# Half of phase 1 woven into the gate scan and the first mixer group of a fused mLSTM-mixer and MoE kernel

## The chip, the cores and the metric

The kernel runs on one core of a Trainium2 chip. The metric is the time of one execution on the device in microseconds. Five instruction queues run side by side and meet only at semaphores: TensorE (PE), VectorE (DVE), ScalarE (ACT), GpSimd (POOL) and the queue that issues the transfers (SP). Each queue executes its instructions in the order in which they were written.

## What is computed

A block of two layers on x of 8 sequences x 1024 tokens x 128 channels, in float32. The first is an mLSTM mixer:

```python
x_mlstm, z = jnp.split(x @ W_up, 2, axis=-1)
x_act = swish(conv4(x_mlstm) + conv_b)               # causal, 4 taps, per channel
q, k, v = headwise(x_act, Wq), headwise(x_act, Wk), headwise(x_mlstm, Wv)
ig, fg = [q, k, v] @ W_ig + b_ig, [q, k, v] @ W_fg + b_fg
lfc = cumsum(log_sigmoid(fg))                        # over the tokens
logD = where(mask, lfc_i - lfc_j + ig_j, -inf);  mD = max(logD, axis=-1)
C = (q @ k.T) * DH ** -0.5 * exp(logD - mD)
h = C / (max(abs(C.sum(-1)), exp(-mD)) + 1e-6) @ v   # 4 heads of 64
h_state = (norm(h) * norm_w + skip * x_act) * swish(z)
x = layernorm(x + h_state @ W_down)
```

The second is an FFN with 16 experts of width 64, of which the 4 best by a sigmoid gate are weighed per token, and a shared expert of width 128: `x = layernorm(x + shared + routed)`.

## The kernel before

The 8192 tokens are cut into 16 groups of G = 512, two to a sequence ("batch" b, "half" f). Four stages follow one another.

**Phase 1** (`phase1`, one function per queue) goes through the 8 batches, 16 halves. SP loads a half of x (`x_in`, L382). PE transposes it into bank 0 (`phase1_xt`, L1190). ACT copies that into `x_hi` and `x_t` (L638, L639), and DVE takes `x_lo = x_t - x_hi` (`x_low`, L815). PE multiplies by W_up in three products each for four blocks of columns (`phase1_up`, L1200 to L1204) into banks 1 to 4. ACT copies the first two into `xm` (L650) and puts the second two through Silu (L673, the gate z). DVE runs the four taps of the convolution on `xm` in pairs of instructions (L835 the first, L838 the others), ACT puts the result through Silu (`phase1_xact`, L628), PE adds the products for the gates into bank 5 (`gate_rows_of`, L1164), and SP stores `xact` (1 MB) and `x_t` to scratch in HBM (L374, L386). On the PE, ACT and DVE queues neighbouring halves overlap: `x_low` of the next half is between the taps of this one.

**The gate scan** runs once over all 8 batches together, on 128 rows (4 chunks x 8 batches x 4 heads). ACT and DVE turn bank 5 into log gates and running sums and maxima (L773 to L778, L852 to L869), PE and DVE carry these from chunk to chunk (L1439 to L1449, L876 to L889), PE spreads the maxima and inter-chunk weights of group 0 over the partitions (L1453, L1462), and three sets of rows go back into token order (`back`, L1434, L902, L904). For the later groups, maxima, weights and decays go through HBM: SP stores them (`store_rows`, L426) and loads them group by group (`load_max`, L404, 1 MB, `load_inter`, L408).

**The groups** (`groups`, L319): `mix(0, None)`, a loop with `mix(g, g - 1)` for g from 1 to 14, `mix(15, 14)`, and `ffn(15)`. `mix(g, f)` carries the mixer of group g beside the FFN of group f. Group 0 has no FFN beside it. In a mixer group POOL makes the arguments of the decay matrices (`args`, L538, L548) and scaled queries (`weigh_queries`, `qs`, L558), ACT exponentiates the former (`decays`, L707), and PE and DVE go through four chunks in a chain: scores times decays on DVE (`weigh_scores`, L934, "C"), keys times weights (`weigh_keys`, L940, "K"), the products of the chunk on PE (`chunk`, L1313 to L1320), the state on DVE (`update_state`, L951, "S"), and POOL's next `kept` (L567). Then come the head scale ("R", L959 to L971, and L580 and L583 on POOL), the head transposes (`head_transposes`, L1329, "H"), the gating by z on DVE (`gate_heads`, L979, L983), the down projection (`down`, L1339, "D"), the sum y (L1008), its statistics and the normalised Y (L1002). `mix_front(g + 1)` prepares keys, values and first scores of the next group. The FFN of a group goes through `ffn_slot(f, j)` for ten slots j; the tables `PE_SLOT` and `DVE_SLOT` (L1483 to L1486) say after which slot each mixer step is issued. The routing takes part of the first slots.

At the first FFN product (L1366) of group 0, PE has `ffn_head`, `key_tokens` and `ffn_logits` of `mix(1, 0)` behind it.

Of the kernel before, what the change touches and what calls it, by code (L numbers as in the profile page):

```python
# [31 lines left out]
F32R = mybir.dt.float32r  # L32
BF16 = mybir.dt.bfloat16
ALU = mybir.AluOpType
# [3 lines left out]
P = 128  # L38
# [5 lines left out]
def mixer_moe_block(nc, x, W_up, conv_w, conv_b, Wq, Wk, Wv, W_ig, b_ig, W_fg, b_fg, norm_w, skip,  # L44
# [18 lines left out]
    QD = Wq.shape[1]  # L63
    assert E == P and INNER == 2 * P and DH == 64 and NH == 4 and HX == 64 and HALVES == 2
# [9 lines left out]
    with ExitStack() as ctx:  # L74
# [81 lines left out]

        p1 = ExitStack()
# [21 lines left out]
        min_f = sb1("min_f", [P, HALVES, P])  # L179
        pre_i = sb1("pre_i", [P, HALVES, P])  # L180
        abs_f = sb1("abs_f", [P, HALVES, P])
        exp_f = sb1("exp_f", [P, HALVES, P])
        log_f = sb1("log_f", [P, HALVES, P])
        p1.close()


        lfc = sb("lfc", [P, HALVES, P])
        rows_a = sb("rows_a", [P, HALVES, P])
        own_max = sb("own_max", [P, HALVES, P])
        run_max = sb("run_max", [P, HALVES, P])  # L190
        ends = sb("ends", [P, 2, HALVES])
        end_rows = sb("end_rows", [R, NC, 2, HALVES])
        carry_rows = sb("carry_rows", [R, CS + 1])
        carry = sb("carry", [P, HALVES])
        neg_end = sb("neg_end", [P, HALVES])
        rows_w = sb("rows_w", [P, HALVES, P])
        rows_floor = sb("rows_floor", [P, HALVES, P])
        rows_inter = sb("rows_inter", [P, HALVES, P])
        rows_decay = sb("rows_decay", [R, CS])
        end_max = sb("end_max", [R, CS])  # L200

# [21 lines left out]
        rows_stored = sem("rows_stored")  # L223
        decay_in = sem("decay_in")
# [3 lines left out]
        x_res = sb("x_res", [P, NC, E])  # L228
        u_sb = sb("u_sb", [P, NC, NH, DV])
        sq = sb("sq", [P, 2, NH, DH])  # L230
        ssq = sb("ssq", [P, NC, NH])
        nrm = sb("nrm", [P, NC, NH])
        nrm1 = sb("nrm1", [P, NC, NH])
        nrm2 = sb("nrm2", [P, NC, NH])
        var_h = sb("var_h", [P, NC, NH])
        r_h = sb("r_h", [P, NC, NH])
        half = sb("half", [P, NC * NH])
        hn = sb("hn", [P, NC, INNER])
        mixed = sb("mixed", [P, NP, G])
        y1 = sb("y1", [P, NC, E])  # L240
        st1 = sb("st1", [P, NC, 6])
        mv1 = sb("mv1", [P, NC, 2])
        ve1 = sb("ve1", [P, NC])
        rs1 = sb("rs1", [P, NC])
        Y = sb("Y", [P, NC, E])
        yT = sb("yT", [P, G])
        yT_hi = sb("yT_hi", [P, G], F32R)
        yT_lo = sb("yT_lo", [P, G], F32R)
        ge = sb("ge", [P, NC, NX])
        ge1 = sb("ge1", [P, NC, NX])  # L250
        gext = sb("gext", [P, NC, NX + TOPK])
        top = sb("top", [P, NC, 8])
        rest = sb("rest", [P, NC, NX + TOPK])
        chosen = sb("chosen", [P, NC, NX])
        csum = sb("csum", [P, NC])
        crec = sb("crec", [P, NC])
        comb = sb("comb", [P, NC, NX])
        comb2 = sb("comb2", [P, NC, 2 * NX], F32R)
        combT = sb("combT", [P, G], F32R)
        s_in = sb("s_in", [P, 2, G])  # L260
        h1 = sb("h1", [P, 2, G])
        h2 = sb("h2", [P, 2, G])
        z2 = sb("z2", [P, NC, E])
        st2 = sb("st2", [P, NC, 6])
        mv2 = sb("mv2", [P, NC, 2])
        ve2 = sb("ve2", [P, NC])
        rs2 = sb("rs2", [P, NC])
        out_sb = sb("out_sb", [P, NC, E])
# [50 lines left out]
        def groups(eng, mix, ffn):  # L319
# [6 lines left out]
            ffn(NG - 1)  # L326

# [13 lines left out]
        def _(sp):  # L341
# [53 lines left out]
            with sp.Fori(FFN_DMAS // HALVES, B - 1) as b:  # L395
                phase1(b)
            phase1(B - 1)
            store_xact(B - 1, 1)

            sp.wait_ge(xt_stored[0], 16 * B)  # L400
            sp.dma_start(xT2[:], xt_d[0]).then_inc(xT_in, 16)
# [13 lines left out]
            sp.wait_ge(xact_stored[0], 16 * B)  # L415
            load_xa(0)
# [6 lines left out]
            def store_rows(dram, rows, s, f):  # L423
                by_chunk = dram.rearrange("(b f) h (k t) -> f k b h t", f=HALVES, k=NC)
                for k in range(NC):
                    sp.dma_start(by_chunk[f, k], rows[k * R:(k + 1) * R, f]).then_inc(s, 16)  # L426

            load_z(0)
            sp.wait_ge(act_scan, SCAN_DECAY_EXP)
            sp.dma_start(decay_d.rearrange("h b c -> b h c"), rows_decay[:]).then_inc(rows_stored, 16)  # L430
            sp.wait_ge(rows_stored, 16)
            for par in range(2):
                for p in range(NP):
                    sp.dma_start(decay[par * DH:(par + 1) * DH, p, :],
                                 decay_d[2 * p + par].rearrange("b c -> (b c)").partition_broadcast(DH)
                                 ).then_inc(decay_in, 16)
# [1091 lines left out]
```

## Time and profile before

| | |
|---|---|
| median of 3 runs | 862.72 us (862.7 to 867.3) |
| profiled execution | 864.57 us, span from first to last instruction 862.8 us |
| mean granted TensorE clock | 0.963 of full speed |
| busy: PE, DVE, ACT, POOL | 787.7, 644.4, 363.7, 371.7 us |
| HBM read, written | 55.24 MB, 25.43 MB |

The page of the profile gives, for the span, each engine's busy time, 40 slices with the granted clock, and groups of instructions. A group of the loop (for instance from one set of transposes L1348 at 219.87 us to the next at 263.68) takes 42 to 44 us. Matmuls overlap and each is drawn with its full duration, so a PE that is drawn busy isn't at its peak; the distance between starts says what one costs in a stream.

### The profile page before, as it was taken

Reading aid. Unit: us, or ns where it says so; the run is one execution under the profiler, and the core shown is the slowest. Engines: PE = TensorE matmul, PEld = TensorE weight load, DVE = VectorE, ACT = ScalarE, POOL = GpSimd, SP = SyncE. Lnnn points to the kernel's source line nnn. Section 1 sums busy time; section 2 is a strip of 40 time slices with the busy share of each in tenths; the row PEclk is TensorE's granted clock in tenths of the full one; section 3 lists DMA queues with packets and bytes.
Section 4 is the critical chain, followed back from the end, with each engine's and each line's share of the span. In section 5 each row is a group of like instructions: output and inputs, shape, how many; then the busy total and the mean of one; then the engine's idle time right before and its main releaser. Section 6 shows DMA issues by size and latency. Waiting matters only on the chain.

```text
span 862.8 us, 17647 instructions
## 1 busy us (share of the span) xinstructions
PE 787.7 (91%) x5783; PEld 666.1 (77%) x5783; DVE 644.4 (75%) x1711; ACT 363.7 (42%) x621; POOL 371.7 (43%) x370
## 2 busy tenths in 40 slices
PE   6888968689999999999999999999999999999976
PEld 5656656578888888888888798888898888888855
DVE  5799953377778777777777877777878777778754
ACT  4757833143434343434343434343434343434131
POOL 5050008553455455454545544545455454543200
PEclk8999977599999999999999999999999999999979
DMA  4887744030404040404040405040404040400000
GB/s 121 237 259 262 288 177 127 30 123 25 135 24 134 24 134 24 134 24 134 24 132 26 134 24 132 26 133 25 134 24 134 24 134 24 134 24 25 1 13 13
DMA packets 53104, 81.01 MB, mean 94 GB/s; under 512 B 10176, under 2 KB 36952, under 8 KB 49112
## 3 DMA queue, kind: packets, MB, share of 16 engines
q1 hardware_dynamic: 53080, 80.68, 30.4%
q8 instruction: 16, 0.26, 0.1%
q14 instruction: 8, 0.07, 0.0%
HBM read 55.24 MB, written 25.43 MB: 93 GB/s over the span
## 4 chain that ended last, share of the span: by engine, by line
PE 45%; DVE 19%; issue 15%; DMA 9%; POOL 6%; ACT 2%; SPq 2%; POOLq 1%; DVEq 1%; ACTq 0%
PE bank L1395 11%; DMA max_b<-max_scratch 8%; PE bank L1366 5%; PE bank L1370 5%; PE bank L1367 5%; DVE acc L838 5%; PE bank L1339 3%; DVE st L990 3%; PE bank L1315 3%; PE bank L1385 3%; PE bank L1313 2%; PE bank L1320 2%; DVE Y L1002 2%; POOL D L548 2%; POOL D L538 2%
## 5 line engine op out<-in xcount | busy, mean ns | idle before, releaser
L754 ACT ACTIVATE s_in<-bank 128x512 f32<-128x512 f32 x144 | 86.1, 598 | 175.9 <-PE bank L1370 174.8
L1395 PEld LDWEIGHTS bank<-ewout,h 128*128 128x128 f32 x1024 | 132.8, 191 | 8.5
L1366 PE MATMUL bank<-yT_hi,in_hi 128*128 128x512 f32 x288 | 128.0, 444 | 8.3 <-DVE h L1097 8.3
L1395 PE MATMUL bank<-ewout,h 128*128 128x128 f32 x1024 | 134.9, 275 | 0.0
L1097 DVE TENSOR_TENSOR h<-s_in,bank 128x512 f32<-128x512 f32 x144 | 98.2, 682 | 49.0 <-PE bank L1370 42.2
L552 POOL TENSOR_TENSOR rs<-ve,half 128x4 f32<-128x4 f32 x32 | 32.6, 1019 | 206.6 <-DVE ve L998 206.6
L1370 PE MATMUL bank<-yT_lo,in_hi 128*128 128x512 f32 x288 | 114.3, 397 | 0.0
L1367 PE MATMUL bank<-yT_hi,in_lo 128*128 128x512 f32 x288 | 113.9, 395 | 0.0
L538 POOL TENSOR_TENSOR D<-a_tok,max_b 128x512 f32<-128x512 f32 x64 | 65.4, 1043 | 110.7 <-DVE max_b L910 67.8
L1101 DVE TENSOR_TENSOR h<-h,bank 128x512 f32<-128x512 f32 x128 | 87.2, 681 | 14.4 <-PE bank L1385 14.4
L951 DVE TENSOR_TENSOR state<-kept,bank 64x130 f32<-64x130 f32 x128 | 36.6, 286 | 59.1 <-PE bank L1320 29.6
L619 ACT ACTIVATE u_sb<-bank 128x260 f32<-128x260 f32 x64 | 24.8, 388 | 131.1 <-PE bank L1315 131.1
L567 POOL TENSOR_TENSOR kept<-state,decay 128x260 f32<-128x260 f32 x64 | 39.7, 620 | 89.0 <-DVE state L951 88.8
L1315 PE MATMUL bank<-vals,C 128*128 128x65 f32 x512 | 73.9, 269 | 0.0
L1366 PEld LDWEIGHTS bank<-yT_hi,in_hi 128*128 128x128 f32 x288 | 55.1, 191 | 20.9 <-DVE h L1097 15.2
L1315 PEld LDWEIGHTS bank<-vals,C 128*128 128x128 f32 x512 | 70.5, 199 | 0.0
L580 POOL TENSOR_TENSOR r_h<-var_h,half 128x8 f32<-128x8 f32 x32 | 52.9, 1653 | 40.2 <-DVE var_h L971 39.1
L838 DVE SCALAR_TENSOR_TENSOR acc<-xm,vecs,acc 128x512 f32<-128x512 f32 x96 | 68.2, 780 | 0.0
L1370 PEld LDWEIGHTS bank<-yT_lo,in_hi 128*128 128x128 f32 x288 | 54.6, 190 | 12.9
L1313 PE MATMUL bank<-state,qs 128*128 128x130 f32 x256 | 56.6, 304 | 7.5 <-issue 5.2
L1367 PEld LDWEIGHTS bank<-yT_hi,in_lo 128*128 128x128 f32 x288 | 55.4, 192 | 5.3
L1313 PEld LDWEIGHTS bank<-state,qs 128*128 128x128 f32 x256 | 41.2, 197 | 16.5 <-issue 15.3
(193 smaller groups left out, 1623.6 us busy)
## 6 DMA issues: line engine op xcount, KB each, us to landing
xact_scratch<-xact SPq DMA_DIRECT2D x16, 1024.0 KB, 4.8
max_b<-max_scratch SPq DMA_DIRECT2D x15, 1024.0 KB, 7.8
xa<-xact_scratch SPq DMA_DIRECT2D x16, 512.0 KB, 6.2
silu_z<-xact_scratch SPq DMA_DIRECT2D x16, 512.0 KB, 3.8
inter_w<-inter_scratch SPq DMA_DIRECT2D x30, 256.0 KB, 7.1
x_in<-in_L_attn_x_dram SPq DMA_DIRECT2D x16, 256.0 KB, 4.8
xt_scratch<-x_t SPq DMA_DIRECT2D x16, 256.0 KB, 4.9
xT<-xt_scratch SPq DMA_DIRECT2D x16, 256.0 KB, 8.2
```

The lines of the kernel that those rows point to most:

```text
L538: pool.tensor_tensor(D[:, kp, par], a_g.rearrange("p k (s two) -> p two k s", two=2)[:, par, 2 * kp:2 * kp + 2] .unsqueeze(3).to_broadcast ...
L580: pool.tensor_tensor(r_h[:, c].rearrange("p k h -> p (k h)"), var_h[:, c].rearrange("p k h -> p (k h)"), half[:, 0:2 * NH], ALU.pow).then_ ...
L754: act.activation(s_in[:, j % 2], bank[4][:], ACT.Silu).then_inc(silu_done, 1)
L838: i = dve.scalar_tensor_tensor(a, src, vecs[:, p, t:t + 1], a, ALU.mult, ALU.add)
L1097: dve.tensor_tensor(dst[:, j % 2], s_in[:, j % 2], bank[5][:], ALU.mult).then_inc(h1_done, 1)
L1101: dve.tensor_tensor(h2[:, (j - 1) % 2], h1[:, (j - 1) % 2], bank[6][:], ALU.mult).then_inc(h2_done, 1)
L1313: pe.matmul(o, qs[:, p, c], state[:, p], start=True, stop=False, skip_group_check=True)
L1315: i = pe.matmul(o[:, par * DV:(par + 1) * DV], C[:, par, kk, p], vals[:, k, 2 * p + par], start=False, stop=True, skip_group_check=True)
L1366: pe.matmul(o, in_hi[:, m, j], yT_hi[:], start=True, stop=False)
L1367: pe.matmul(o, in_lo[:, m, j], yT_hi[:], start=False, stop=False)
L1370: pe.matmul(o, in_hi[:, m, j], yT_lo[:], start=False, stop=True).then_inc(done, 1)
L1395: i = pe.matmul(bank[7][:, k * P:(k + 1) * P], h2[:, j % 2, k * P:(k + 1) * P], w, start=(j == k == 0), stop=(j == NJ), skip_group_check=True)
```

## The change

Phase 1 as it was now runs over the first EARLY = 4 batches only. The other eight halves are "late halves" h = 0 to 7. Their instructions are written by hand into the queues of the scan and of `mix(0)`:

- DVE: a late half is five steps (tap 0, `x_low` of the next half, taps 1 to 3), 40 in all. `late(n)` issues the next n: 3 ahead of the scan, 1, 4, 2, 1 and 3 between its parts, then 1 ahead of the first keys, 14 ahead of the steps of `mix(0)` by `LATE_STEPS`, 5 ahead of the head gating, 6 ahead of y.
- PE: `late_first(h)` (transposes of half h + 1 into bank 7, first two products of half h), `late_second(h)` (the other two) and `late_gates(h)`. All four products of a half use the two banks 4 and 6 in turn.
- ACT: `late_xm`, `late_xt`, `late_xact` and `late_z`.
- SP: `late(h)`: load of a half of x, stores of `x_t` and `xact`, between the transfers of `mix(0)`.

The scan runs twice, first over batches 0 to 3, of which groups 0 to 7 are made; the second pass (s = 1) is spread out: the gate rows after y of group 0, chunk scans in slot 3 of group 1, ends in slot 5, carry in slots 6 and 7, the exponentials at the end of group 1, and the rows back in slot 5 of group 2, with the stores by SP there. Groups 0, 1 and 2 are written out ahead of the loop, which goes from 3 to 14. Banks of the scan's small results move. Tiles that live beyond phase 1 no longer share memory with it; this changes no instruction.

The core of the diff (the functions of the scan are cut out of the old text and get a parameter s; those lines are left out):

```diff
+    EARLY = B // 2
+    LATE = HALVES * (B - EARLY)
...
-            mix(0, None)
-            with eng.Fori(1, NG - 1) as g:
+            for g in range(SCAN_GROUPS):
+                mix(g, g - 1 if g else None)
+            ready()
+            with eng.Fori(SCAN_GROUPS, NG - 1) as g:
                 mix(g, g - 1)
...
+        # SP
+            late(0, False)
+            sp.wait_ge(xt_stored[0], 16 * EARLY)
+            sp.dma_start(xT2[:], xt_d[0]).then_inc(xT_in, 16)
+            sp.wait_ge(xact_stored[0], 16 * EARLY)
             load_xa(0)
             load_z(0)
+            sp.dma_start(x_res[:], x_g[0]).then_inc(x_res_in, 16)
+            store_xact(EARLY - 1, 1)
+            late(1, False)
+            store_decay(0)
+            store_maxima(0, 1)
+            late_xact(1)
+            load_decay(0)
+            late(2)
+            store_maxima(0, 0)
...
+                    elif isinstance(g, int) and g == 2:
+                        store_decay(1)
+                        store_maxima(1, 0)
+                        store_maxima(1, 1)
+                        load_decay(1)
...
+        # ACT
+            late_xm(0)
+            late_xt(0)
+            late_z(0)
+            late_xact(0)
             act.preload_act_table_set("natural_log_exp_and_others")
+            scan_gates(0)
+            late_xm(1)
+            scan_ends(0)
+            late_xt(1)
+            scan_rows(0)
             act.wait_ge(max_mm, 1)
             for h in (2, 3):
                 copy(max_b[:, h], bank[(1, 2, 3, 0)[h]][:]).then_inc(max_in, 4)
+            late_z(1)
             act.wait_ge(inter_mm, 1)
+            copy(inter_w[:, 0], bank[3][:]).then_inc(inter_in, 16)
+            late_xact(1)
+            late_xm(2)
             mix_front(0)
             decays(0)
+            late_xt(2)
+            late_xact(2)
+            late_z(2)
...
+            def late_steps(k):      # k == NC: after the loop over the slots
+                if k == 0:
+                    late_xm(3)
+                elif k == 1:
+                    late_xt(3); late_xact(3); late_z(3)
+                elif k == 2:
+                    late_xm(4); late_xt(4); late_xact(4); late_z(4)
+                elif k == 3:
+                    late_xm(5)
+                else:
+                    late_xt(5); late_xact(5); late_z(5)
+                    late_xm(6); late_xt(6); late_xact(6); late_z(6)
+                    late_xm(7); late_xact(7); late_z(7); late_xact(8)
+                    scan_gates(1)
...
+        # DVE
+            late(3)
+            scan_gates(0)
+            scan_chunks(0)
+            late(1)
+            scan_carry(0)
+            scan_maxima(0)
+            back(0, 0)
+            late(4)
             dve.wait_ge(max_mm, 1)
             for h in (0, 1):
                 dve.tensor_copy(max_b[:, h], bank[(1, 2, 3, 0)[h]][:]).then_inc(max_in, 4)
+            late(2)
+            back(0, 1)
+            back(0, 2)
+            late(1)
             dve.wait_ge(inter_mm, 1)
+            dve.tensor_copy(inter_w[:, 1], bank[0][:]).then_inc(inter_in, 16)
+            late(3)
...
+        # PE
+            late_first(0)
+            phase1_gates_x(EARLY - 1, 1)
+            phase1_gates(EARLY - 1, 0)
+            late_second(0)
+            phase1_gates(EARLY - 1, 1)
+            late_first(1)
...
+            scan_ends(0)
+            back(0, 0)
+            late_gates(1)
+            scan_carry(0)
...
             i.then_inc(max_mm, 1)
+            late_second(1)
+            back(0, 1)
+            back(0, 2)
...
             i.then_inc(inter_mm, 1)
+            late_first(2)
             mix_keys(0)
             mix_values(0)
+            late_gates(2)
+            late_second(2)
...
+            def late_steps(what, arg):
+                if (what, arg) == ("C", 0):
+                    late_gates(3); late_second(3)
+                elif (what, arg) == ("C", 1):
+                    late_first(4)
+                elif (what, arg) == ("K", 1):
+                    late_gates(4); late_second(4)
+                elif (what, arg) == ("C", 2):
+                    late_first(5)
+                elif (what, arg) == ("C", 3):
+                    late_gates(5); late_second(5); late_first(6)
+                elif what == "H":
+                    late_gates(6); late_second(6)
+                elif (what, arg) == ("D", 1):
+                    late_first(7); late_gates(7); late_second(7)
...
+LATE_UP = (4, 6)
+LATE_STEPS = {("S", 0): 3, ("S", 1): 2, ("C", 1): 2, ("K", 1): 2, ("S", 2): 1, ("S", 3): 4, ("H", None): 5}
+SCAN_GROUPS = 3
+SCAN_CHUNKS_SLOT, SCAN_ENDS_SLOT, SCAN_CARRY_SLOT, SCAN_MAX_SLOT, SCAN_BACK_SLOT = 3, 5, 6, 7, 5
```

In the excerpt several calls are put on one line, some waits are left out, and the lines "# SP" and the like name the queue. On PE, `late_first(3)` is ahead of the first chunk of `mix(0)`, behind `key_tokens`. `late_up` waits for a bank to be free, `late_xt(h)` is the copy of the transposes of half h + 1, and `late_xact(h)` is the Silu after the taps of half h - 1.

## Rows read from the trace of the kernel before

**Rows 1.** Busy time by stage: window, length, engines (instructions), granted clock, DMA.

```profile
70.00:114.00 44.00, 40.11 (x529) 28.33 (x527) 44.00 (x73) 32.63 (x64) 0.00 (x0) 0.98 0.77 275
114.00:179.00 65.00, 45.66 (x303) 38.70 (x304) 26.82 (x76) 20.13 (x39) 32.09 (x34) 0.68 0.38 121
179.00:222.00 43.00, 41.39 (x289) 35.75 (x290) 32.69 (x93) 17.93 (x29) 21.68 (x21) 1.00 0.10 29
```

**Rows 2.** Chain of waits, whole span (start, length, what): two batches of phase 1.

```profile
87.28 0.92 DVE acc L835 x2
88.79 2.74 DVE acc L838 x5
98.26 0.92 DVE acc L835 x2
```

**Rows 3.** Timeline of PE (start, duration): one half of phase 1.

```profile
88.48 0.66 PE L1190 MATMUL bank<-ident,x_in 128*128 128x128 f32 x4
88.89 0.48 PE L1200 MATMUL bank<-x_hi,up_hi 128*128 128x512 f32 x1
...
90.45 0.64 PE L1164 MATMUL bank<-x_t,g_pad 128*32 128x128 f32 x16
91.02 0.50 PE L1200 MATMUL bank<-x_hi,up_hi 128*128 128x512 f32 x1
...
92.62 1.08 PE L1164 MATMUL bank<-xact,g_pad 128*32 128x128 f32 x32
```

**Rows 4.** Timeline of ACT, the scan.

```profile
114.82 1.28 ACT L768 ACT_TABLE_LOAD   x1
...
128.06 1.09 ACT L619 ACTIVATE max_b<-bank 128x512 f32<-128x512 f32 x2 [5.08 <-PE bank L1453]
```

**Rows 5.** Chain of waits from 100 to 180 us.

```profile
113.60 1.21 ACT xact L628 x2
...
121.77 0.49 DVE run_max L888 x2
...
122.30 5.67 PE bank L1453 x32
...
138.91 0.46 PE bank L1313 x2
...
158.53 0.29 DVE state L951
```

**Rows 6.** Timeline of PE: the first FFN product of group 0.

```profile
178.85 0.47 PE L1366 MATMUL bank<-yT_hi,in_hi 128*128 128x512 f32 x1
```

**Rows 7.** Windows of 2 us, PE: busy time, then the granted clock.

```profile
116.00:118.00 2.00, 0.00 (x0) 0.50 1.14 352
126.00:128.00 2.00, 2.00 (x19) 0.96 0.11 26
140.00:142.00 2.00, 1.87 (x9) 0.50 0.95 244
```

**Rows 8.** Timeline of POOL: arguments and queries of group 0.

```profile
129.51 2.04 POOL L538 TENSOR_TENSOR D<-a_tok,max_b 128x512 f32<-128x512 f32 x2 [67.77 <-DVE max_b L910]
...
132.71 2.38 POOL L558 TENSOR_TENSOR qs<-xa,inter_w 128x1024 f32<-128x1024 f32 x1
```

**Rows 9.** Timeline of DVE: scan, copies of max_b, sum y of group 0.

```profile
117.64 0.74 DVE L859 TENSOR_TENSOR_SCAN lfc<-min_f,log_f 128x128 f32<-128x128 f32 x2
...
128.07 1.29 DVE L910 COPY max_b<-bank 128x512 f32<-128x512 f32 x2 [4.89 <-PE bank L1453]
...
170.89 0.69 DVE L1008 TENSOR_TENSOR y<-bank,x_res 128x512 f32<-128x512 f32 x1 [3.75 <-PE bank L1339]
```

**Rows 10.** Timeline of DVE in phase 1 while POOL works.

```profile
55.82 3.11 DVE L815 TENSOR_TENSOR x_lo<-x_t,x_hi 128x512 fp32r<-128x512 f32 x1
58.86 6.45 DVE L838 SCALAR_TENSOR_TENSOR acc<-xm,vecs,acc 128x512 f32<-128x512 f32 x6
```

**Rows 11.** Timeline of POOL in the same stretch.

```profile
55.59 5.85 POOL L525 TENSOR_TENSOR in_lo<-in_w,in_hi 128x1152 fp32r<-128x1152 f32 x2
```

More of the change, by code:

```diff
@@ L437, in _ @@
[L437 to L448 removed]
+                    r = k * R + part * n
@@ L452, in mix @@
             def mix(g, f):
+                first = isinstance(g, int) and g == 0
+                if isinstance(g, int) and g == 1:
+                    for i in range(HALVES):
+                        sp.wait_ge(xt_stored[i], 16 * B)
+                        sp.wait_ge(xact_stored[i], 16 * B)
                 sp.wait_ge(arg_sub, nth(g, 4, 3))
@@ L466, in mix @@
                     load_z(g + 1)
+                    if first:
+                        late(7)
                 if f is not None:
@@ L783, in _ @@
-            act.wait_ge(dve_scan, SCAN_MAX)
-            for f in range(HALVES):
-                act.activation(rows_inter[:, f], run_max[:, f], ACT.Exp, scale=-1.0, bias=carry[:, f:f + 1]
-                               ).then_inc(act_scan, 1)
+            scan_gates(0)
[3 more added lines that the diff above has]
+            scan_rows(0)
             act.wait_ge(max_mm, 1)
@@ new lines, in phase1, with late @@
+                    tap(b, f, 0)
+                    if f == 0:
+                        x_low(b, 1)
+                    else:
+                        x_low(b + 1, 0)
+                    for t in range(1, TAPS):
+                        tap(b, f, t)
+            late_done = [0]
+            def late(n):
+                for _ in range(n):
+                    h, step = divmod(late_done[0], TAPS + 1)
+                    late_done[0] += 1
+                    b, f = late_half(h)
+                    if step == 1:
+                        if h < LATE - 1:
+                            x_low(*late_half(h + 1))
+                    else:
+                        tap(b, f, step - (step > 1))
@@ L903, in back @@
+            def back(s, n):
+                dve.wait_ge(back_mm, 2 * BACK if s else n + 1)
+                d = (a_tok, w_tok, floor_tok)[n][:].rearrange("p b f k h -> p f k b h")
+                rows = back_bank(s, n)[:, 0:CS * R].rearrange("p (f k b h) -> p f k b h", f=HALVES, k=NC, b=B)
+                for f in range(HALVES):
+                    if n == 2:
+                        j = dve.tensor_scalar(d[:, f, :, batches(s)], rows[:, f, :, batches(s)], EPS_MIX, None, ALU.add)
                     else:
-                        j = dve.tensor_copy(d[:, f], s[:, f])
+                        j = dve.tensor_copy(d[:, f, :, batches(s)], rows[:, f, :, batches(s)])
@@ L1018, in mix_front, with scan_steps @@
                 weigh_scores(g, 0)
+            def scan_steps(g, j):
+                if g == 1 and j == SCAN_CHUNKS_SLOT:
+                    scan_chunks(1)
+                elif g == 1 and j == SCAN_CARRY_SLOT:
+                    scan_carry(1)
+                elif g == 1 and j == SCAN_MAX_SLOT:
+                    scan_maxima(1)
+                elif g == 2 and j == SCAN_BACK_SLOT:
+                    for n in range(BACK):
+                        back(1, n)
             def mix(g, f):
+                first = isinstance(g, int) and g == 0
+                if first:
+                    late(1)
                 weigh_keys(g, 0)
@@ L1033, in mix @@
                                 if arg is not None else gate_heads(g)
+                if first:
+                    late(6)
                 mixer_out(g)
+                if first:
+                    assert late_done[0] == LATE * (TAPS + 1)
+                    scan_gates(1)
                 if f is not None:
@@ L1211, in phase1 @@
                         phase1_xt(b, 1)
-                    elif not first and not last:
+                    elif not first:
                         phase1_xt(b + 1, 0)
@@ L1413, in mix @@
                 key_tokens(g, 0)
+                if first:
+                    late_first(3)
                 if f is not None:
@@ L1497 @@
 SCAN_INTER = 7
+ACT_SCAN = 10
 BACK = 3
```

617 lines of the change are left out of this document (385 added, 232 removed).

## The prediction

> **What bounds the kernel now.** I read the stage windows first, then the chain of waits from the last batch of phase 1 to the first FFN matmul, then the timelines of single engines there. The kernel has three regimes [rows 1]. From 70 to 114 us, the last four batches of phase 1, DVE is busy for 44.00 of 44 us: the convolution taps set the pace, one batch of two halves per 10.98 us, 5.49 us a half, its taps following one another at 0.55 us (five in 2.74) [rows 2]. From 114 to 179 us (the gate scan and mixer group 0, with no FFN beside it) no engine is full: DVE 26.82 of 65 us, PE 45.66, and much of that at the low clock. From 179 us the groups are full of PE work (41.39 of 43 us). So 38 us of DVE idleness stand beside 44 us of DVE work that group 0 does not need. The change tries to pour the second into the first.
>
> **What is removed.** Eight halves of phase 1 leave the stretch in which they are alone: 8 x 5.49 = 43.9 us [rows 2]. The last half of a batch now has an x_low in it, 0.6 us, which the last of all has not, so the taps of the fourth batch end 43.3 us before those of the eighth do, at 70.3 instead of 113.6 [rows 5]. I call this moment T in both kernels.
>
> **What a late half costs on each engine.** PE [rows 3]: transposes 0.41, first two up products 1.56, gate rows from x 0.57, second pair 1.6, gate rows from xact 1.08 us: 5.2 us at 2.4 GHz, 42 us for eight. DVE: 0.92 for the first tap pair, 0.6 for x_low (from 88.20 to 88.79), 3 x 1.1 for the rest: 4.8 [rows 2]. ACT: four pairs like the 1.09 us of the max_b pair [rows 4], 4.4 us. DMA: the same transfers over a longer time. The sums of the stage are then 26.8 + 8 x 4.8 = 65 us on DVE, and on PE 42 plus between half and all of its present 45.66 (much of that is at 1.2 GHz), 65 to 88, say 75, against the present 43.3 + 65.3 = 108.6 us from T to the first FFN matmul. The sums alone allow a gain near 33 us. But each half goes PE, ACT, DVE, ACT, PE; four in-order queues carry it in a written order, now in the same two product banks (4 and 6) for all four products of a half; and each link can hold back the mixer instruction behind it. So I walk the queues, with T = 0. The times after are mine, from these durations; those before are read from [rows 5, 6, 9], less 113.6.
>
> - *To run_max.* Before 8.2. After: ACT has the second pair of half 0 ahead of the last xact, so the scan begins 1.6 us later; DVE does a pair of taps in the scan's gap. 10.6: +2.4.
> - *To max_b copied.* Before 15.8. The 32 broadcasts take 5.67 us because they start at 1.2 GHz (granted 0.50 at 116, full by 126 [rows 7]) after PE stood idle between two gate groups. After, late products fill that hole and I take 3.7 us; DVE's four queued steps delay its copies by 1 us. 16.6: -1.6 for the stage.
> - *To the first chunk, C0.* Before 25.3. After, POOL's first two arguments end at 19.9. Its qs waits for DVE's copy of inter_w, which stands behind the first tap of half 2, which waits for ACT's xm, which waits for PE (up products behind the inter broadcasts): 23.0. qs (2.4 us) and the other arguments (3.2, as from 129.51 to 132.71) [rows 8] end at 28.6, their exponentials at 29.3, and only then does ACT come to late_xt(2). DVE's late(3) stands ahead of mix_front(0) and needs exactly that x_t for x_low: DVE is idle for 7 us, to 30.4. Then x_low, two tap pairs, vals and the C pair: 35.1. PE meanwhile waits 5 us, falls to 1.2 GHz as it does now after idling, and does key_tokens, late_first(3) and C0 at that rate. C0 at 39: +12.9 for the stage. This is where most of the overlap is lost.
> - *C0 to the last state.* Before 19.9 (25.3 to 45.2). After, each later chunk has one or two up-product blocks before it (1.6 us of PE each), and S, C and K on DVE have 14 steps of about 1 us among them, of which two x_low wait until ACT has evacuated u. I get 29.4 (39 to 68.4): +9.5.
> - *Last state to y.* Before 12.1; after, the last taps of half 5 and four steps of half 6 stand ahead of the head gating, and the rest of half 6 and half 7 ahead of y, the last half waiting for its up products behind D: 20.0 (y at 88.4): +7.9.
> - *y to the first FFN matmul.* Before 8.0. After, scan_gates(1) stands between y and Y on DVE and waits for ACT's last xact, the gate rows and an activation table load (1.28 us [rows 4]); decays(1) and the evacuations of keyT come after it on ACT. 11.5 (to 99.9): +3.5.
>
> Sum: 2.4 - 1.6 + 12.9 + 9.5 + 7.9 + 3.5 = 34.6 us back of 43.3, net -8.7.
>
> **The second scan.** Its DVE part, without the gate rows counted above, is about 6 us: from 117.64 [rows 9] to the end of run_max at 122.26 [rows 5] are 4.6 us with 0.9 of waiting, and the floor and three back copies come on top. Its 14 transposes and small matmuls add 1.5 us of PE to groups that have PE busy for 41.39 of 43 us. Slot 3 of a group has no DVE room, the others some. Between 0 (all hidden) and 7.5 (all shown, DVE and PE) I take the middle, 4. SP's 21 extra issues in group 2 stand behind load_inter and ahead of load_xa, which is needed only at the group's end: 0. Peeling two iterations: 0, between -1 and +1, for I find no pause at the loop's edge to take away.
>
> **A cost between engines.** At 55.8 us one x_low took 3.11 us and at 58.9 six taps 6.45, while POOL ran its two in_lo subtractions, 5.85 us [rows 10, 11]; alone they take 0.6 and 3.3 [rows 2]. So 5.6 us were lost to 5.85 of POOL: POOL instructions with SBUF inputs hold up DVE ones with two SBUF inputs. The rest of phase 1 ran with POOL idle; now the taps meet 32 us of POOL work [rows 1]. If a third of it meets taps, DVE loses 10 us, some of it in waits that exist anyway. Not in the walk: between 0 and 10, I take 1, because the longest POOL runs (the arguments and qs of group 0) fall mostly in DVE's 7 us wait. The Trainium skill (SBUF — State Buffer, Who interferes with whom) says that the shared ports are held for a whole instruction and the loser blocks fully; the trace's 3.11 us agrees. By that rule, applied to all 32 us, the sum would end near the time before; this is rival C.
>
> Total: -8.7 + 4 + 1 = -3.7 us. The profiled execution took 864.6 us (span 862.8); less 3.7 is 860.9, and as the median of the runs is 1.9 us lower, 859.0 as a median. I say **859**.
>
> **Rivals.**
> A. *The overlap works.* The wait of DVE for late_xt(2) is short and the steps between S, C and K fall into DVE's idle time. For it: DVE has 38 us idle there, and the PE clock may stay up. Against it: the order of the queues above. With half the gap between the walk's 34.6 us given back and the sums' 10 us (a stage of 75), 22 come back: 864.6 - 43.3 + 22 + 5 gives 848, **846** as a median.
> B. *Slower: the low clock.* PE stays at 1.2 GHz from C0 to the end of D, as it does now from 140 on although it is busy most of the time [rows 7]. Then five late halves of 5.2 us of PE work cost 10.4 each: +26, of which the walk's idle PE time hides about 8: 861 + 18 = 879, **877**. It decides once PE is low for more than some 15 of those 50 us.
> C. *The gain goes to the shared port.* 10 us instead of 1: 870, **868**, within 1%.
>
> **Numbers.** Forecast 0.40, A 0.33, B 0.12, C 0.12, something else 0.03. A measurement of this kernel tells a change of about 1% (8.6 us) from none. Faster by over 1% (below 854.1): A and a tenth of the forecast's case: 0.37. Slower (above 871.4): B, the rest and a fifth of C: 0.17. Within: 0.46. The range leaves out the better part of A and most of B: 843 to 871; the forecast's own is 851 to 867.
>
> **What would show it.** T at 70 us; run_max 10 us and C0 39 us after it; a DVE wait of some 7 us on ACT's x_t before vals of group 0; a PE clock of 0.5 around C0; y 88 us and the first FFN matmul 99 us after T; groups 1 and 2 together 4 to 5 us longer than two others; taps of 1 to 3 us beside POOL instructions. C0 before 32 us is A; a granted clock of 0.5 for most of C0 to D is B. The prediction is wrong if one of these moves by over 8 us, or if an SP wait (the xact stores stand ahead of store_maxima and load_xa) delays a load that I count as early.

## The result and the profile after

| | before | after |
|---|---|---|
| median of 4 runs each, side by side | 864.51 us | 886.92 us |
| profiled execution, span | 862.8 us | 886.0 us |
| mean granted TensorE clock | 0.963 | 0.966 |
| busy: PE, DVE, ACT, POOL | 787.7, 644.4, 363.7, 371.7 us | 790.5, 659.4, 355.0, 375.4 us |

The changed kernel is slower: ratio 1.0226, interval 1.0176 to 1.0275. The forecast of 859 and its range to 871 missed it, on the side of rivals B and C, but for neither's reason alone. The kernel before took between 864.5 and 871.6 us as a median beside the different runs below, and the changed kernel was timed only here; so an experiment is compared with the changed kernel by the stage times of the profiles, and its ratio stands for itself.

Busy time by stage of the changed kernel (columns as in [rows 1]):

```profile
70.00:114.00 44.00, 33.52 (x323) 26.38 (x321) 30.96 (x64) 27.81 (x52) 13.23 (x14) 0.88 0.47 160
114.00:149.00 35.00, 25.77 (x274) 21.10 (x272) 25.04 (x45) 16.17 (x32) 15.05 (x14) 0.95 0.67 205
149.00:174.00 25.00, 15.36 (x186) 12.56 (x186) 15.21 (x26) 6.99 (x14) 5.56 (x3) 0.80 0.33 125
174.00:190.00 16.00, 9.74 (x78) 7.56 (x79) 8.04 (x22) 10.99 (x19) 3.15 (x3) 0.89 0.55 199
```

No engine is full in any of the four stretches; DVE (the third pair, after PE and PEld) was busy for 44.00 of 44 us in phase 1 before. The work was moved into DVE's idle time, and a new idle time grew around it. The prediction's T, 113.6 in the kernel before, is 3.53 us after the start of the last six taps (110.07), when the first Silu behind them can start. The last six early taps start at 68.03 in the changed kernel, so T is 71.6 there. From these the stages compare as follows, each as its growth over before:

| stage | forecast | measured | ends after at |
|---|---|---|---|
| T to run_max | +2.4 | +4.0 | 83.73 (start) |
| to max_b copied | -1.6 | +0.3 | 91.67 |
| to C0 | +12.9 | +12.4 | 113.57 |
| to the last state | +9.5 | +15.0 | 148.45 |
| to y | +7.9 | +13.6 | 174.11 |
| to the first FFN product | +3.5 | +7.5 | 189.54 |
| sum | +34.6 | +52.7 | |

52.7 us came back for 42.0 removed (the sums are of unrounded times), where 34.6 of 43.3 were forecast. From one set of transposes of Y to the next, group 1 took 48.42 us (43.28 before) and group 2 44.99 (43.81): the second scan shows 6.3 us, where 4 was taken. Groups 3 to 15 took 43.49 on average against 42.99, 6.5 us in all; of those e1 and e7 below tell. Sums: 52.7 - 42.0 + 6.3 + 6.5, and 0.3 at the tail, is 23.8; the spans differ by 23.2, the rest is that the first line ends at the FFN product and the others start at the transposes.

**Where the forecast was right.** Ahead of C0 DVE, ACT and PE wait for one another as walked. DVE and ACT, then PE:

```profile
105.68 0.87 DVE L974 TENSOR_TENSOR x_lo<-x_t,x_hi 128x512 fp32r<-128x512 f32 x1 [7.36 <-ACT x_t L687]
```
```profile
105.66 1.28 ACT L696 ACT_TABLE_LOAD   x1
```
```profile
109.95 1.09 PE L1555 MATMUL bank<-ident,keyT 128*128 128x128 f32 x4 [5.23 <-DVE vals L1123]
```

DVE stands 7.36 us (7 forecast) on the x_t that ACT makes only after the exponentials of D, and PE waits 5.23 us behind it (5 forecast). One term on the way there was wrong: the late products did not keep the clock up for the 32 broadcasts of the maxima. PE waits 2.05 us ahead of the scan's transposes at 81.41, the granted clock is 0.50 from 84 to 88 us, and the broadcasts take 6.01 us, where 3.7 were taken and 5.67 measured before.

**What the walk had not seen.** Four things, in order of time.

First, SP. The chain of waits of the changed kernel from 108 to 124 us:

```profile
108.58 0.69 SPq L452
...
113.28 0.62 SPq L452
113.94 1.75 DMA inter_scratch<-rows_inter
115.84 0.34 SPq L433
116.22 7.78 DMA x_in<-in_L_attn_x_dram
124.04 0.66 PE bank L1412 x4
```
```profile
124.04 0.66 PE L1412 MATMUL bank<-ident,x_in 128*128 128x128 f32 x4 [2.07 <-DMA x_in<-in_L_attn_x_dram]
```

The load of x for late half 5 is issued at 116.22. It stood behind the store of an xact that waited for ACT (108.13), eight stores of the scan's rows (0.6 to 0.7 us each), the wait that they have landed, and the load of max_b; it then took 7.78 us beside the 1 MB of max_b. PE waited 2.07 us for it here; e5 to e7 show a wait of over 7 us once the links ahead of it are shorter. The walk gave SP no stage of its own: it listed a delayed load under what would make it wrong, and the sum has no term for it.

Second, DVE beside POOL. DVE, then POOL:

```profile
131.49 4.68 DVE L989 SCALAR_TENSOR_TENSOR acc<-xm,vecs,acc 128x512 f32<-128x512 f32 x4
136.09 0.68 DVE L1138 TENSOR_TENSOR keys<-bank,w_tok 128x512 f32<-128x512 f32 x1
```
```profile
131.06 2.49 POOL L606 TENSOR_TENSOR D<-a_tok,max_b 128x512 f32<-128x512 f32 x2 [3.79 <-DVE C L1132]
133.51 2.12 POOL L616 TENSOR_SCALAR_AFFINE_SELECT D<-D 128x512 f32<-128x512 f32 x2
```

Four taps take 4.68 us where four take 2.73 when POOL is idle (at 145.10), the keys stand behind them, and PE waits 3.58 us for the keys at 136.83. All taps of L989 together are busy for 75.3 us against 68.2 before.

Third, the head part. PE, DVE, ACT:

```profile
153.38 1.97 PE L1593 MATMUL bank<-ident,hn 128*128 128x128 f32 x8 [5.62 <-POOL hn L651]
155.28 1.08 PE L1386 MATMUL bank<-x_t,g_pad 128*32 128x128 f32 x16
...
164.01 3.62 PE L1603 MATMUL bank<-w_down,mixed 128*128 128x128 f32 x16 [4.76 <-DVE mixed L1181]
```
```profile
157.88 0.69 DVE L974 TENSOR_TENSOR x_lo<-x_t,x_hi 128x512 fp32r<-128x512 f32 x1 [5.71 <-ACT x_t L687]
```
```profile
156.76 0.60 ACT L687 ACTIVATE x_hi<-bank 128x512 fp32r<-128x512 f32 x1 [8.37 <-PE bank L1386]
```

ACT may overwrite x_t only after PE has read it for the gate rows of half 5 (L1386 at 155.28). Those products are queued behind the head transposes, which wait for POOL's hn. So hn holds x_lo of the next half, which holds taps, which hold `mixed`, which holds D. PE falls to the low clock in its two idle stretches (granted 0.80 in this stage). D takes 3.62 us, much as in the kernel before, where it ran at the low clock too:

```profile
167.29 3.56 PE L1339 MATMUL bank<-w_down,mixed 128*128 128x128 f32 x16 [2.14 <-DVE mixed L983]
```

Fourth, table loads, and keyT behind them. ACT, then PE and DVE:

```profile
176.61 1.28 ACT L906 ACT_TABLE_LOAD   x1
178.34 1.28 ACT L908 ACT_TABLE_LOAD   x1
180.07 1.28 ACT L775 ACT_TABLE_LOAD   x1
```
```profile
184.66 2.08 PE L1546 MATMUL bank<-xa,keyT 64*128 64x128 f32 x16 [5.03 <-ACT keyT L687]
```
```profile
186.81 1.29 DVE L1132 TENSOR_TENSOR C<-bank,D 128x512 f32<-128x512 f32 x2 [6.45 <-PE bank L1546]
```

One load of 1.28 us was in the walk; there are three. The first scan's code asks for a table with both functions ahead of the scan, the second pass doesn't, so Exp, Ln and the exponentials of D each bring their own.

And in group 1, where the second scan's carry is. DVE, POOL, PE:

```profile
216.50 2.44 DVE L1060 TENSOR_TENSOR_SCAN carry_rows<-end_rows,carry_rows 32x4 f32<-32x4 f32 x2
```
```profile
216.33 2.34 POOL L626 TENSOR_TENSOR qs<-xa,inter_w 128x1024 f32<-128x1024 f32 x1
```
```profile
218.99 0.24 PE L1748 MATMUL bank<-carry_rows,ident 32*32 32x2 f32 x8 [1.47 <-DVE carry_rows L1060]
223.74 0.50 PE L1630 MATMUL bank<-yT_hi,in_hi 128*128 128x512 f32 x1 [1.79 <-DVE run_max L1077]
```

Two scans of 32x4 elements took 2.44 us in place of 0.46 (the first pass, at 82.59), as long as POOL's qs ran, and PE waited twice.

### The profile page after: what moved, and what is told of

It reads as the page before. It is cut to its first block, busy times and chain, and to the rows that moved or that the text cites. A ratio compares the mean times of both kernels' runs of the same rounds, so it can differ in the third digit from the quotient of the medians.

```text
span 886.0 us, 17398 instructions
## 1 busy us (share of the span) xinstructions
PE 790.5 (89%) x5805; PEld 668.1 (75%) x5805; DVE 659.4 (74%) x1735; ACT 355.0 (40%) x623; POOL 375.4 (42%) x370
## 4 chain that ended last, share of the span: by engine, by line
PE 43%; DVE 17%; DMA 13%; issue 12%; POOL 6%; ACT 4%; SPq 4%; POOLq 1%; DVEq 0%; ACTq 0%
DMA max_b<-max_scratch 11%; PE bank L1659 10%; PE bank L1630 5%; PE bank L1634 5%; PE bank L1631 4%; PE bank L1603 3%; DVE st L1188 3%; PE bank L1649 3%; DVE acc L989 2%; POOL D L616 2%; POOL D L606 2%; PE bank L1593 2%; DMA x_in<-in_L_attn_x_dram 2%; DVE Y L1200 2%; PE bank L1577 2%
## 5 line engine op out<-in xcount | busy, mean ns | idle before, releaser
L1630 PE MATMUL bank<-yT_hi,in_hi 128*128 128x512 f32 x288 | 128.2, 445 | 12.9 <-DVE h L1319 11.1
L989 DVE SCALAR_TENSOR_TENSOR acc<-xm,vecs,acc 128x512 f32<-128x512 f32 x96 | 75.3, 844 | 0.0
L1577 PE MATMUL bank<-vals,C 128*128 128x65 f32 x512 | 71.2, 262 | 0.0
L1577 PEld LDWEIGHTS bank<-vals,C 128*128 128x128 f32 x512 | 67.3, 191 | 0.0
L1575 PE MATMUL bank<-state,qs 128*128 128x130 f32 x256 | 54.8, 296 | 9.0 <-issue 8.0
```

Of the source, the lines that this page charges most:

```text
L989: i = dve.scalar_tensor_tensor(a, src, vecs[:, p, t:t + 1], a, ALU.mult, ALU.add)
L1575: pe.matmul(o, qs[:, p, c], state[:, p], start=True, stop=False, skip_group_check=True)
L1577: i = pe.matmul(o[:, par * DV:(par + 1) * DV], C[:, par, kk, p], vals[:, k, 2 * p + par], start=False, stop=True, skip_group_check=True)
L1630: pe.matmul(o, in_hi[:, m, j], yT_hi[:], start=True, stop=False)
```

## The experiments

The start of `min_f` (78.27 after, 116.73 before) marks a run's own start-up, which differs by some us between executions. "Stage" below is the time from it to the transposes of Y of group 0: 59.9 before, 108.4 after.

**e1: the written-out groups alone.** Kernel before, groups 0 to 2 written out ahead of the loop.

```diff
-            mix(0, None)
-            with eng.Fori(1, NG - 1) as g:
+            for g in range(3):
+                mix(g, g - 1 if g else None)
+            with eng.Fori(3, NG - 1) as g:
```

> The kernel before with groups 0 to 2 written out ahead of its loop, nothing else changed. The changed kernel's groups 3 to 15 take 6.5 us more in all than those of before, 0.5 each. If writing out groups (longer code, other loop bounds) does that, this kernel is 5 to 8 us slower than before. If it is the landing of the max_b load (8.1 us median in the changed kernel, 7.8 before), which varies from execution to execution, this kernel is within 2 us of before.

Ratio 0.9965 (0.9919 to 1.0011). Groups 3 to 15 take 43.34 us on average in its profile, again above the 42.99 of before, with a time that isn't longer. In e11 and e12, whose groups are those of the kernel before, they take 43.34 and 43.55. So the 6.5 us of the loop groups are mostly the scatter of one execution, not the new shape of the program. In e1 a group's period (42.0 to 44.5 us) goes with how long POOL waits for max_b: 44.5 where it waits 4.97 us, 42.0 where it waits 0.61.

**e2: no second scan in groups 1 and 2.** The changed kernel without chunk scans, carry, maxima, exponentials and rows back of pass 1; the gate rows stay. The tokens of batches 4 to 7 get rows of batches 0 to 3.

```diff
-                if g == 1 and j == SCAN_CHUNKS_SLOT:
-                    scan_chunks(1)
...
-                elif g == 2 and j == SCAN_BACK_SLOT:
-                    for n in range(BACK):
-                        back(1, n)
```

> The changed kernel without the second scan pass in groups 1 and 2 (chunk scans, ends, carry, maxima, rows back, their exponentials); its gate rows at the end of group 0 stay. Tokens of batches 4 to 7 get the rows of batches 0 to 3, so part of the computation is left out. Groups 1 and 2 take 6.3 us more than before in the changed kernel. If that is the second pass, this one is 5 to 7 us faster than the changed kernel and group 2 is back at 43 to 44 us; if it is the low clock and the late start of group 1 after the stage, it gains under 3 us and group 1 stays above 46 us.

Ratio 1.0129 (1.0051 to 1.0207). Transposes of Y at 186.65 as with the scan; group 1 43.50 us, group 2 43.91. The second scan costs 4.9 and 1.1, 6.0 us, as the first of the two expectations has it; most of the loss lies ahead of it.

**e3: gate rows of half 5 ahead of the head transposes.**

```diff
                     late_first(6)
+                    phase1_gates_x(*late_half(5))
                 elif what == "H":
-                    late_gates(6)
+                    phase1_gates(*late_half(4))
```

> The changed kernel, but PE adds the gate rows from x_t of half 5 ahead of the head transposes of group 0 and not behind them. In the trace ACT waits 8.4 us for these (they free x_t), DVE then 5.7 us for ACT's x_t, and the head gating of group 0 stands behind that. Theory 'order of the queues': 4 to 6 us faster. Rival 'amount of work' (ports, PE clock and the sum of work set the length, so a wait that is taken away comes back elsewhere): under 1.5 us.

Ratio 1.0078 (1.0035 to 1.0121), stage 103.8: 4.6 us less. x_lo of half 6 now runs at 151.60 with no wait, y at 169.12 in place of 174.11. The third link is shown. Not all of it is kept: the four taps behind this x_lo now run beside POOL's hn and qs and take 5.62 us for 2.73, and group 1 takes 50.18 us for 48.42.

**e4: one table load for the second pass.**

```diff
             def scan_gates(s):
+                if s:
+                    act.preload_act_table_set("natural_log_exp_and_others")
```

> The changed kernel with one table load ahead of the gate rows of the second pass, with Exp and Ln in one table. In the trace ACT does three loads of 1.28 us there (before exp_f, before log_f, before D) and PE waits 5.0 us for keyT behind them. Theory 'order of the queues': the three become one, which hides in ACT's wait for the gate rows: 3 to 4 us faster. Rival 'amount of work': under 1.5 us, since Y of group 0 or the low clock takes over.

Ratio 1.0109 (1.0071 to 1.0148), stage 103.1: 5.3 us less. ACT:

```profile
175.62 1.28 ACT L901 ACT_TABLE_LOAD   x1
176.92 0.47 ACT L905 ACTIVATE abs_f<-bank,b_f 128x256 f32<-128x256 f32 x1
177.43 0.42 ACT L908 ACTIVATE exp_f<-abs_f 128x256 f32<-128x256 f32 x1
```

The one load that is left stands where ACT waits for the last gate rows anyway, so three loads, 3.84 us, leave the path. PE shows most of the rest:

```profile
181.48 1.16 PE L1548 MATMUL bank<-xa,keyT 64*128 64x128 f32 x16 [1.09 <-ACT keyT L687]
```

It waits 1.09 us for keyT in place of 5.03, keeps the full clock, and the 16 products take 1.16 us in place of 2.08. The Trainium skill (ScalarE: Activation LUTs, What ACT_TABLE_LOAD costs) gives a load 1.28 us, as here, plus about 1.4 us of draining; in the changed kernel the exponential ends at 178.32 and the next load starts at 178.34, so no such drain shows.

**e5: DVE's wait ahead of C0 taken away.** `mix_front(0)` and the first keys go ahead of four late steps, and `late_first(3)` behind C0.

```diff
-            late(3)
...
-                if first:
-                    late(1)
                 weigh_keys(g, 0)
+                if first:
+                    late(4)
```

> The changed kernel with the tap steps taken from ahead of vals, C and keys of group 0: mix_front(0) and weigh_keys(0) go first on DVE, late_first(3) behind C0 on PE, late_xm(3) behind the first u on ACT, and the steps ahead of S0 later (none, 3, 2, 2, 3, 4, 5). In the changed kernel DVE waits 7.4 us for ACT's x_t there and C0 starts 41.6 us after the last early tap. Theory 'order of the queues': C0 at 35 us and the kernel 4 to 7 us faster than the changed one (ratio to before near 1.015). Rival 'amount of work': C0 is early but the tap steps, now packed into the chunks, take it back; y stays where it is and the kernel gains under 1.5 us.

Ratio 1.0179 (1.0123 to 1.0235), stage 107.1: 1.3 us less, the size of the rival. The wait of 7.36 us is gone (DVE waits 2.29 for vals) and C comes at 103.27 instead of 109.73, yet the end of the stage hardly moves: PE now waits 7.7 us for x of half 5, 2.07 in the changed kernel. The 7 us that the walk named as "where most of the overlap is lost" are not to be had by themselves, since the same load is late behind them. What they are worth once it comes early no run tells, for e9 has both.

**e6: the three together,** with the chunk scans in slot 4 in place of 3.

> The changed kernel with the gate rows of half 5 first, one table load, the front of group 0 first, and the chunk scans of the second pass in slot 4 (not 3) of group 1. The single steps took 5.0 and 4.1 us off the stage before group 1. Theory 'order': they add up to 12 to 16 us, so the kernel is 3 to 8 us slower than before. Rival: they overlap and give 8 us at most.

Ratio 1.0044 (1.0015 to 1.0073), stage 96.6: 11.8 us less (4.6, 5.3 and 1.3 alone add to 11.2), so the three add up. Group 1 is no better (49.96). The largest waits left, PE and DVE:

```profile
121.61 1.12 PE L1414 MATMUL bank<-ident,x_in 128*128 128x128 f32 x4 [7.90 <-DMA x_in<-in_L_attn_x_dram]
```
```profile
126.21 1.29 DVE L1134 TENSOR_TENSOR C<-bank,D 128x512 f32<-128x512 f32 x2 [9.11 <-issue]
```

**e7 and e8: max_b loaded half a group earlier,** in e6 and in the kernel before. In both, SP loads max_b of group g + 2 as soon as the last arguments of g + 1 are made:

```diff
                     load_xa(g + 1)
+                    if not (isinstance(g, int) and g == NG - 2):
+                        sp.wait_ge(arg_sub, nth(g, 4, 7))
+                        load_max(g + 2)
```

> The four orders and, besides, SP issues load_max(g + 2) in group g as soon as POOL has read max_b, and not behind the output store and x_res of the next group. Groups take 42.1 us where the load lands in time and 43 to 45 where POOL waits for it. If that wait sets the difference, all groups come to 42.1 to 42.4 us and the kernel is 12 to 16 us faster than with the four orders alone; if it is absorbed, under 3 us.

> The kernel before with the early load_max alone (and groups 14 and 15 written out). Its groups take 43.1 us in the mean and 42.1 where the load lands within 7.8 us. Theory 'the load sets the excess': 12 to 14 us faster than before, groups at 42.1 to 42.3. If another wait takes over, under 4 us.

e7: ratio 1.0016 (0.9986 to 1.0046), median 868.45 beside e6's 871.94; every period from group 3 to 14 is 43.0, and POOL no longer waits for the DMA there. e8: ratio 0.9946 (0.9912 to 0.9980), some 4.7 us, periods of groups 2 to 14 from 43.0 to 43.1, where 42.1 was expected. That the landing makes the scatter is shown; neither expected gain came. DVE in e8:

```profile
319.16 0.69 DVE L1089 CAST comb<-comb 128x64 fp32r<-128x64 f32 x1
319.89 1.00 DVE L1091 TENSOR_TENSOR comb<-comb 128x64 fp32r<-128x64 f32 x1
```

These took 0.20 and 0.23 in the kernel before (315.74), where POOL was idle. POOL's arguments now start at 318.77 and fall on them, ahead of a product that waits for `comb`, 0.76 us. The scatter is gone; that this meeting is what keeps the periods from 42.1 is likely, not shown.

**e9: the loads ahead of the stores on SP.** e7, with the loads of halves 5, 6 and 7 ahead of the stores of xact, and max_b of group 1 ahead of the row stores of the even half.

```diff
-            late(2)
+            late(2, False)
+            late_x(3)
+            sp.wait_ge(max_stored, 16 * NC)
+            sp.wait_ge(arg_sub, 4)
+            load_max(1)
+            late_xact(2)
             store_maxima(0, 0)
```

> e7_changed_max_early with the SP queue of the stage reordered: the loads of late halves 5, 6 and 7 are issued ahead of the stores of xact that stand before them, and the load of max_b for group 1 ahead of the stores of the even half's maxima. In e7 the load of half 5 was issued at 115.81, and PE waited for it 7.84 us at 114.9; POOL waited 8.93 us for max_b (issued at 115.43), DVE stood for 9.20. If those waits came from the order on SP: PE's wait for x_in below 2 us, first Y transposes of group 0 near 167 (e7 174.5), span 857 to 860, ratio near 0.993. Rival, that the shared port and the steps of the chain set the pace in this stretch: the waits return at the next link, first Y transposes not before 172, span 863 or more.

Ratio 0.9899 (0.9863 to 0.9935), stage 90.2: 6.4 us less than e7. The load of half 5 is issued at 100.68 and PE no longer waits for any x_in; the transposes of Y start at 168.0, near the 167 of the first expectation. The loads of x and that of max_b, for which POOL waited 8.9 us in e7, were moved together, and what each gave wasn't separated. What is left of DVE's waits above 3 us is one:

```profile
135.22 0.69 DVE L992 TENSOR_TENSOR x_lo<-x_t,x_hi 128x512 fp32r<-128x512 f32 x1 [3.36 <-ACT x_t L702]
```

**e10: PE's part of the second scan behind the FFN products of its slot.** e9, with the two parts taken from ahead of the products and put here; the second now waits for the copy of the carry, no longer for run_max:

```diff
                     if f is not None:
                         ffn_slot(f, j)
+                    if isinstance(g, int) and g == 1 and j == SCAN_ENDS_SLOT:
+                        pe.wait_ge(u_out[NC - 1], g + 1)
+                        scan_ends(1)
+                    elif isinstance(g, int) and g == 1 and j == SCAN_MAX_SLOT + 1:
+                        pe.wait_ge(dve_scan, DVE_SCAN + SCAN_MAX - 1)
```

> e9 with PE's two parts of the second scan in group 1 moved from ahead of the FFN products of their slot to behind them (ends behind slot 5's, the wait for the carry copy behind slot 8's). In e7 PE waited 2.49 us for ends at 200.48 and ran the next products at the low clock (0.60 instead of 0.39 us each, some 1.5 us), and 1.67 us for run_max at 213.09. If the cost of the second scan is these waits: the period of group 1 falls from 50 to 44.5 us, span 5 to 6 us below e9's, ratio near 0.987. Rival, that it is DVE's and PE's added work in full groups: group 1 stays above 47 us and the waits come back at other products.

Ratio 0.9844 (0.9807 to 0.9882), the fastest of all: median 856.50 beside 870.11 of before. In the profiled run 3.5 us of its 7.8 over e9 are a shorter start-up (`min_f` at 74.31 instead of 77.82), 1.5 the stage, where nothing was changed, and 2.8 group 1, now 47.05 us. Neither theory holds whole: the two waits on PE are gone, but everything shifted and DVE's carry met POOL's qs again:

```profile
193.20 2.45 DVE L1078 TENSOR_TENSOR_SCAN carry_rows<-end_rows,carry_rows 32x4 f32<-32x4 f32 x2
195.68 0.16 DVE L1082 TENSOR_TENSOR end_max<-carry_rows,end_rows 32x8 f32<-32x8 f32 x1
```

**e11 and e12: the price of POOL beside DVE, by itself.** Kernel before, with 16 POOL instructions more in phase 1, where DVE is full and nobody waits for POOL.

```diff
+            pool.memset(D[:, 1], 1.0).then_inc(beside, 1)
+            for n in range(16):
+                pool.wait_ge(beside, n + 1)
+                pool.tensor_tensor(D[:, 0, n % 2], D[:, 1, 0], D[:, 1, 1], ALU.subtract).then_inc(beside, 1)
```

In e12 the last line is `pool.tensor_scalar(D[:, 0, n % 2], D[:, 1, 0], 2.0, None, ALU.mult)`.

> The kernel before, with 16 more POOL instructions right after the in_lo subtractions (from 61.4 us), each a subtraction of two 128x512 SBUF tiles into a third (about 1.02 us each by the pair L538, 16.3 us in all), whose results nobody reads. In this stretch DVE is full with taps and x_low (5.49 us a half), POOL otherwise idle, and nothing waits for POOL. If a POOL instruction with two SBUF inputs holds up DVE's for its whole length: the last early tap, run_max and everything behind move by 14 to 16 us, taps of 0.68 us beside them show 1.5 us and more; span 877 to 879, ratio 1.017. Rival, that each delays only the DVE instruction under way (a third, as the four taps of 4.68 us for 2.73 in the changed kernel's stage suggest): +5 us, ratio 1.006. If the 3.11 us of x_lo at 55.8 us had another cause: +0.

> As e11_pool_two_inputs, but each of the 16 POOL instructions reads one tile (times a constant), like the multiplication by skip in L572 and the mask of L543. If one SBUF input on POOL doesn't hold up DVE's two: +0 to +1 us, ratio 1.000 to 1.001, taps stay at 0.68 us. Rival, that any POOL instruction on SBUF does: as in e11, in proportion to its length (some 0.8 us each by L572, 12 to 13 us in all).

e11: ratio 1.0192 (1.0123 to 1.0260). DVE, then POOL:

```profile
59.00 10.51 DVE L844 SCALAR_TENSOR_TENSOR acc<-xm,vecs,acc 128x512 f32<-128x512 f32 x6
69.43 2.89 DVE L841 TENSOR_SCALAR acc<-xm,vecs 128x512 f32<-128x512 f32 x2
72.24 1.75 DVE L821 TENSOR_TENSOR x_lo<-x_t,x_hi 128x512 fp32r<-128x512 f32 x1
73.91 10.18 DVE L844 SCALAR_TENSOR_TENSOR acc<-xm,vecs,acc 128x512 f32<-128x512 f32 x6
```
```profile
62.56 25.45 POOL L532 TENSOR_TENSOR D<-D 128x512 f32<-128x512 f32 x16
```

From 59.00 to 88.49 DVE did two halves' work, 10.98 us at 5.49 a half: 18.5 lost, 2.4 of them to the end of in_lo as in [rows 10]. So 16 instructions of 1.02 us of POOL cost DVE 16 us, and the transposes of Y come 17.2 us later, as the first expectation has it. The two engines took turns: the half from 69.43 to 84.01 has nine DVE instructions and takes 14.58 us, 9.1 more than 5.49, one POOL instruction for each of them, the one-input first taps (2.89 for 0.99) too. The trace thus agrees with the rule of the Trainium skill (SBUF — State Buffer, Who interferes with whom) that the loser blocks for the whole instruction.

e12: ratio 1.0046 (1.0005 to 1.0088). DVE, then POOL:

```profile
69.56 5.11 DVE L844 SCALAR_TENSOR_TENSOR acc<-xm,vecs,acc 128x512 f32<-128x512 f32 x6
74.60 1.43 DVE L841 TENSOR_SCALAR acc<-xm,vecs 128x512 f32<-128x512 f32 x2
75.95 0.68 DVE L821 TENSOR_TENSOR x_lo<-x_t,x_hi 128x512 fp32r<-128x512 f32 x1
```
```profile
61.13 27.87 POOL L532 TENSOR_SCALAR D<-D 128x512 f32<-128x512 f32 x16
```

A half takes 6.99 us in place of 5.49, for four halves: some 6 us. One input costs DVE far less than two but not nothing, and this is no lock for a whole instruction: four POOL instructions a half cost DVE 1.5 us. POOL took 1.74 us for each, and 1.57 for one like it (L573) in the kernel before, not the 0.8 of the expectation. Neither expectation for e12 had that size.

## Why the prediction was wrong

- **T and the removed time.** 71.6 for 70.3: the eight halves gave 42.0 us in place of 43.3. Start-up scatter (2.9 us between e9 and e10 in DVE's longest wait for x_t alone) can cover this; 1.3 us.
- **To C0: near in size (+16.7 for +13.7), wrong in weight.** The last early Silu starts 3.5 us after T (75.12), behind two more pairs of half 0 on ACT, where 1.6 was taken, and the broadcasts kept the low clock. The DVE wait was there, but e5 shows that taking it away alone gains 1.3 us. A wait on a walk is a loss only if nothing later is late anyway, and x of half 5 was.
- **C0 to the last state: +15.0 for +9.5.** The failed step is that the sum has no term for SP here: the walk followed four queues and not the fifth. In the changed kernel SP's stores, in written order ahead of the load of half 5, held PE for 2.07 us on the chain, and four taps beside POOL took 1.95 us more than alone, on the chain as well: 4.0 beside the 5.5 that the walk was short here. With the other orders mended (e5 to e7) the late loads held PE for 7.7 to 7.9 us and DVE for 9.1 to 9.2, and e9 gives 6.4 back.
- **Last state to y: +13.6 for +7.9.** The failed step is a missing link: x_t has two readers, and the second was queued behind the head transposes. e3 gives 4.6 back.
- **y to the first FFN product: +7.5 for +3.5.** The term "an activation table load (1.28)" was mis-sized: three loads stood there, 3.84 us, and the low clock behind them; e4 gives 5.3 back.
- **The sum.** The walk had 34.6 for 52.7, 18.1 short. The gains of e9, e3 and e4 add to 16.3, but that they come so near is partly luck: e4 also takes out the load that the walk had counted, and e9's gain was measured where PE waited 7.84 us for the load and not 2.07. The changed kernel with the order on SP alone was not run.
- **Second scan: 4 taken, 6.0 measured (e2),** inside its bounds of 0 and 7.5. Part of it is carry behind qs, 2.0 us on DVE.
- **Port contention: 1 taken, of 0 to 10.** The taps lost 7.1 us of DVE time. The mechanism of rival C is shown by e11, at the full rate of one to one; how much of the 7.1 is on the path wasn't isolated beyond the 1.95 us above, for POOL's work of group 0 can't be taken away without its readers. It is inside the growth of the stages above and no further term.
- **Rival B, the low clock, is out.** The granted clock from C0 to the last state was 0.95, and 0.80 from there to y; in the kernel before it was 0.52 in both. So the stages grew although their clock rose, and D took what it took before.
- **Rival A was closer to reach than it seemed:** with the queues reordered, the transposes of Y start 94.4 us after T (e10, where the last six early taps start at 65.10), 63.0 before and 115.1 in the changed kernel. Then 31.4 us come back for 42.0, and the kernel is 1.6% faster than before. 0.5% of that is to be had without the change (e8).
- **Loop groups: 0 taken.** Right as far as e1, e11 and e12 tell: 6.5 us of the profiled span were scatter.

## What to carry to other kernels

When work is woven into a stage that waits, walk every in-order queue, the one that issues transfers first: put each load as early as its buffer is free and stores behind it. List for each moved instruction all readers of the buffer that it overwrites and where the last of them is queued. And add to each DVE instruction that runs beside POOL's two-input ones the length of one of these (1.02 us in e11), to the one-input first taps too: idle DVE time beside a busy POOL isn't free time for taps.

## What the hardware showed beyond what was expected

- POOL subtractions with two SBUF inputs delayed DVE one to one (16.3 us of them, 16 us lost), and made POOL's own 16 take 25.45 us. The small ones suffer most in proportion: two carry scans of 0.46 us took 2.44 beside qs, `comb` 1.00 in place of 0.23.
- One-input POOL instructions cost DVE 1.5 us per half, both on its two-input taps (5.11 for 4.05) and on its one-input ones (1.43 for 0.99), while x_low stayed at 0.68.
- A 1 MB broadcast of max_b lands 4.8 to 9.0 us after its issue in the kernel before, and each group's period moves with it. Issued half a group earlier the periods are equal to 0.1 us, at 43.0: not the shortest that had been seen, 42.1.
